# Last pass of a two-layer kernel: the stores of the result move from the sync engine's queue to ScalarE's

## The chip, the cores and the metric

The kernel runs on one core of a Trainium2 chip, as one launch. The metric is its device time in microseconds. All times called "us" below are of that kind; "ns" is marked.

## The reference, cut to what matters

The input `x` is (8, 512, 128, 128) float32, 256 MB, and so is the output.

```python
# layer 0: a 3x3 stride-2 grouped convolution, a gate per channel cluster, then upsampling back
x1 = conv(sx, w_down)                       # (8, 256, 64, 64), "downsampled" in the kernel
labels = kmeans(x1[0]); mu, var = gmm(mean over each cluster); y = sigmoid(...)
up = repeat((1 + y[:, slabel]) * x1, 2, axis=1) * w_up
x = bilinear_up_x2(up) + sx
# layer 1: linear attention in a basis P of 64 cosine products, with norms lamdq, lamdk, lamdv
xP = x P;  WqxP, WkxP, WvxP = Wq xP, Wk xP, Wv xP
out = WvxP @ ((A fatt PT/lamdq + rowsum) / lamdv) + out_bias
return gamma * out + x
```

All that is large in the last pass is: read x again, read the downsampled image, compute per 4 rows of the picture one product that carries both the upsampled image and the attention's result, add x and a shift per channel, and write the result.

## The kernel before

There are four passes, one after another. The first reads x, convolves it with VectorE and projects it with TensorE. Two short ones compute clusters and the mixture, and work out the gates. The last, `second_pass`, begins at some 2070 us. All of the change is in it.

The last pass goes over 8 batches. Each has `UNITS` = 32 units of 4 rows, and a unit is 1 MB of x, read into one of `XBUF` = 8 slots `second_x` by two DMAs of 512 KB, changed in place, and stored by two DMAs of 512 KB. Two units make a chunk of 8 rows, for which 4 to 6 rows of the downsampled image (`second_dd`) are read. Every engine has its own instruction stream, written out by hand; `batches` runs `step(b, u, more)` for every unit, in a loop over seven batches and then once more, unrolled, for the last (there `more` is False). Engines are tied only by semaphores. What each does for unit u:

- The sync engine's queue (SP), `step` at line 1026: on odd u the rows of a later chunk (`load_rows`), then `store(b, u)`, then `load_image` of unit u + 6 (`AHEAD`), which waits on `y_out`, that is until the slot's last store (that of unit u - 2) has landed. `store` (line 1010) waits until VectorE has added the last of four banks of u.
- ScalarE, `step` at line 1299: `stage` (for a few u, small steps of the next batch's attention: copies, a square root at u = 15); on odd u `weight(b, m + 2, 0)`, eight ACTIVATEs (L1257) that interpolate vertically for the chunk after next; `copy(b, u + 1)` (L1278, L1281, L1282), which copies transposed rows from PSUM for GpSimd and the right-hand factor for TensorE; on odd u `weight(b, m + 2, 1)`, eight more. `weight` with 0 waits for the interpolation of an earlier chunk (`interpolated`), since it writes a part buffer that VectorE has read.
- GpSimd: scales the copied rows by the gates into half of the left factor (L964, `second_left`), which TensorE waits for at its first product of the next unit.
- TensorE: four groups of 8 matmuls (L1172) into four PSUM banks `second_o`, one per bank; after the first the transposes of unit u + 1 (L1142, `second_mid_t`), after the second those of L1155; then `stage`, the matmuls of the next batch's attention (none in the last batch).
- VectorE, `step` at line 1465, an order that matters here. `add` n (L1417) takes bank n and adds it to x in the slot. The order is `add` 0, `scale_odd` of unit u + 1 (L964), `add` 1, on even u `frequencies` (L1408), `add` 2, on even u `interpolate` (L1399), `add` 3, then `stage`. So on even units the interpolation is ahead of the last add, whose semaphore `store` waits for. On odd units there is no interpolation.

Of the kernel before, what the change touches and what calls it, by code (L numbers as in the profile page):

```python
# [9 lines left out]
B, C, H, W = 8, 512, 128, 128  # L10
P = 128
T, S = 2, 2
# [36 lines left out]
FREE = 1  # L49
# [823 lines left out]
HALF = ROWS2 // 2  # L873
UNITS = H // HALF
PAIRS = HALF // 2
BANKS = TS
XBUF = 8
# [14 lines left out]
def second_pass(nc, x, cst, p_sb, r_sb, inter, wqk_sb, wv_sb, vx, gam, xd, xps, coef, out):  # L892

    xv = x.rearrange("b (t g s) h w -> b t g s (h w)", t=T, s=S)
    ov = out.rearrange("b (t g s) h w -> b t g s (h w)", t=T, s=S)
    with Scope(nc, "second") as sc:
        xt = [sc.sb(f"x{i}", [P, T, S, HALF, W]) for i in range(XBUF)]
# [30 lines left out]
        y_out = [sc.sem(f"y_out{i}") for i in range(XBUF)]  # L928
# [8 lines left out]
        added = [sc.sem(f"added{i}") for i in range(BANKS)]  # L937
# [20 lines left out]
        def chunk_of(u):  # L958
            return u // 2
# [10 lines left out]
        def batches(eng, step, prologue=None):  # L970

            if prologue:
                prologue()
            with eng.Fori(0, B - 1) as b:
                for u in range(UNITS):
                    step(b, u, True)
            for u in range(UNITS):
                step(B - 1, u, False)

        with nc.Block() as block:  # L980
            @block.sync
            def _(sp):
                def load_rows(b, m):

                    slot, n = m % 2, m % CH2

                    sp.wait_ge(weighted, b * CH2 + m + CHUNK_LEAD - 1)
                    batch = b + m // CH2
                    rows = xd[batch].rearrange("t g n -> g t n")
                    first, last = max(n * DROWS - 1, 0), min(n * DROWS + DROWS + 1, HD)  # L990
                    at = first - (n * DROWS - 1)
                    if n == 0:
                        sp.dma_start(dd[slot][:, :, 0, :], rows[:, :, 0:WD]).then_inc(dd_in[slot], 16)
                    if n == CH2 - 1:
                        sp.dma_start(dd[slot][:, :, HALO - 1, :], rows[:, :, (HD - 1) * WD:HD * WD]
                                     ).then_inc(dd_in[slot], 16)
                    sp.dma_start(dd[slot][:, :, at:at + last - first, :].rearrange("g t h w -> g t (h w)"),
                                 rows[:, :, first * WD:last * WD]).then_inc(dd_in[slot], 16)

                def load_image(b, u, free=True):  # L1000
                    i = u % XBUF
                    if free:

                        sp.wait_ge(y_out[i], (b * (UNITS // XBUF) + u // XBUF) * T * 16 + Y_LEAD)
                    for t in range(T):
                        sp.dma_start(xt[i][:, t, :, :, :].rearrange("g s h w -> g s (h w)"),
                                     xv[b + u // UNITS, t, :, :, u % UNITS * HALF * W:(u % UNITS + 1) * HALF * W]
                                     ).then_inc(x_in[i], 16)

                def store(b, u):  # L1010
                    i = u % XBUF
                    sp.wait_ge(added[BANKS - 1], b * UNITS + u + 1 + FREE)
                    for t in range(T):
                        sp.dma_start(ov[b, t, :, :, u * HALF * W:(u + 1) * HALF * W],
                                     xt[i][:, t, :, :, :].rearrange("g s h w -> g s (h w)")).then_inc(y_out[i], 16)

                def prologue():
                    load_rows(0, 0)
                    load_rows(0, 1)
                    for u in range(AHEAD):  # L1020
                        load_image(0, u, free=False)
                    load_rows(0, 2)
                    for i in range(XBUF):
                        sp.sem_inc(y_out[i], Y_LEAD)

                def step(b, u, more):
                    if u % 2 == 1 and (more or chunk_of(u) < CH2 - 3):
                        load_rows(b, chunk_of(u) + 3)
                    store(b, u)
                    if more or u + AHEAD < UNITS:  # L1030
                        load_image(b, u + AHEAD)

                batches(sp, step, prologue)
                for i in range(XBUF):
                    sp.wait_ge(y_out[i], B * UNITS // XBUF * T * 16 + Y_LEAD)
# [181 lines left out]
            def _(act):  # L1217
# [22 lines left out]
                def weight(b, m, e):  # L1240


                    c, n = m % 2, m % CH2
                    if e == 0:
                        if c == 0:
                            loads = (m // CH2) * (CH2 // 2 + 1) + n // 2 + 1 + 1
                        else:
                            loads = (m // CH2) * (CH2 // 2 + 1) + n // 2 + 1 + (n == CH2 - 1)
                        act.wait_ge(dd_in[c], b * (CH2 // 2 + 1) * 16 + loads * 16)

                        act.wait_ge(mid_turned, (b * CH2 + m) * 2 - 2 + TURN_LEAD)
                        if m > 0:

                            act.wait_ge(interpolated, b * CH2 + m)
                    for r in range(2):
                        for i in range(DROWS):
                            last = nc.scalar.activation(  # L1257
                                (mid[c], part)[r][:, :, 2 * i + 1 - e, :], dd[c][:, :, e + r + i, :], ACT.Copy,
                                scale=row_w[:, 2 * e + r, n * DROWS + i:n * DROWS + i + 1])
                    if e == 1:  # L1260
                        last.then_inc(weighted, 1)

                def place_vt(b, u):

                    a = u % 2
                    act.wait_ge(multiplied, (b * UNITS + u) * BANKS - BANKS + UNIT_LEAD)
                    act.wait_ge(vt_made, b + u // UNITS + 1)
                    for rows, e in ((lo, 0), (hi, 1)):
                        last = nc.scalar.activation(left[a][rows, e:HALF:2, :, :].rearrange("p h n g -> p h (n g)"),
                                                    vt[rows, :].unsqueeze(1).broadcast_to([UV, PAIRS, C]), ACT.Copy)  # L1270
                    last.then_inc(vt_placed, 1)

                def copy(b, u):

                    a = u % 2
                    act.wait_ge(mid_turned, b * UNITS + u + 1 + TURN_LEAD)
                    act.wait_ge(left_made[1], b * UNITS + u + FREE)
                    nc.scalar.activation(mid_copy[hi, :, :, :], mid_t[hi, :, :, :], ACT.Copy).then_inc(mid_copied, 1)  # L1278
                    act.wait_ge(zt_turned, b * UNITS + u + 1 + TURN_LEAD)
                    act.wait_ge(multiplied, (b * UNITS + u) * BANKS - BANKS + UNIT_LEAD)  # L1280
                    nc.scalar.activation(right[a][lo, 0:HALF:2, :], zt_t[lo, 0:PAIRS, :], ACT.Copy)  # L1281
                    nc.scalar.activation(right[a][hi, 1:HALF:2, :], zt_t[hi, 0:PAIRS, :], ACT.Copy  # L1282
                                         ).then_inc(right_made, 1)
                    if u % UNITS < 2:
                        place_vt(b, u)

                def prologue():
                    for b in range(B):
                        act.wait_ge(coef_turned, b + 1)
                        nc.scalar.activation(coef_all[:, b, :], zt_t[:, :, :].rearrange("p n g -> p (n g)"), ACT.Copy  # L1290
                                             ).then_inc(coef_copied, 1)
                    for m in range(2):
                        for e in range(2):
                            weight(0, m, e)
                    for u in range(UNITS):
                        stage(0, u)
                    copy(0, 0)

                def step(b, u, more):
                    m = chunk_of(u)  # L1300
                    if more:
                        stage(b + 1, u)
                    ahead = u % 2 == 1 and (more or m + 2 < CH2)
                    if ahead:
                        weight(b, m + 2, 0)
                    if more or u < UNITS - 1:
                        copy(b, u + 1)
                    if ahead:
                        weight(b, m + 2, 1)

                batches(act, step, prologue)

            @block.vector
# [287 lines left out]
```

## Time and profile before

| | us |
|---|---|
| median of 3 runs | 3865.55 (3852.54 to 3874.26) |
| the profiled execution, its own time | 3863.4 |
| its span | 3861.8 |
| PE busy in the span | 3209.1 (83%) |
| DVE busy | 3018.2 (78%) |
| ACT busy | 1871.3 (48%) |
| POOL busy | 645.3 (17%) |
| second_x stores, KB each | 512 DMAs, 512.0 KB, 5.7 us to landing |
| second_x loads, KB each | 512 DMAs, 512.0 KB, 7.5 us to landing |

PE is TensorE, PEld its weight loads, DVE VectorE, ACT ScalarE, POOL GpSimd, SP the sync engine. A letter q behind an engine (SPq) means its instruction queue: a DMA shows there as long as its issue takes, not as long as the data travel. "A releaser" is what ended an engine's idle time. Busy shares are averages over passes with different limits, so the last pass has to be read by itself.

### The profile page before, as it was taken

The page shows a single profiled execution, that of the slowest core. Times are in us where ns is not written, and L with a number is a line of the kernel's source. Part 1 is how long each engine was busy: PE and PEld are TensorE (multiplying, and loading weights), DVE is VectorE, ACT ScalarE, POOL GpSimd, SP SyncE. Part 2 cuts the span into 40 slices and gives each one's busy share as a digit, 9 for nine tenths or more (in the row PEclk, how much of TensorE's full clock was granted, in tenths as well). Part 3 has the DMA queues.
Part 4 walks back from the last instruction along what each step waited for, and adds up shares of the span by engine and source line. Part 5 has one row for each costly group of instructions (what it writes and reads, how often), then busy time and mean ns, then how long its engine had stood idle before and what let it go on. Part 6 is the DMA issues. An engine that isn't in the chain of part 4 may idle for free. (4 is left out here: it accounts for less than half of the span.)

```text
span 3861.8 us, 68816 instructions
## 1 busy us (share of the span) xinstructions
PE 3209.1 (83%) x23738; PEld 2390.1 (62%) x23738; DVE 3018.2 (78%) x3491; ACT 1871.3 (48%) x4272; POOL 645.3 (17%) x325
## 2 busy tenths in 40 slices
PE   7999999999999745998556887888889887888877
PEld 3454554545455345776334787877778787877777
DVE  5999999999999933113443897979889797979877
ACT  4555555555555310222221555555655556555654
POOL 0000000000000000000000333333333333333333
PEclk9999999999999865998666999999999999999999
DMA  6646556556556212221002899999999999999998
GB/s 275 254 201 259 243 206 264 231 219 264 220 231 265 116 73 98 102 116 44 0 0 78 289 345 322 348 327 346 346 340 343 326 343 337 343 325 347 353 349 305
DMA packets 348925, 945.54 MB, mean 245 GB/s; under 512 B 25937, under 2 KB 58833, under 8 KB 329490
## 3 DMA queue, kind: packets, MB, share of 16 engines
q1 hardware_dynamic: 339346, 907.41, 63.3%
q0 software_dynamic: 9216, 33.56, 2.1%
q8 instruction: 194, 3.18, 0.3%
q14 instruction: 169, 1.38, 0.1%
HBM read 638.90 MB, written 301.99 MB: 244 GB/s over the span
## 5 line engine op out<-in xcount | busy, mean ns | idle before, releaser
L189 DVE SCALAR_TENSOR_TENSOR first_acc<-first_x,first_wd,first_acc 128x1024 f32<-128x1024 f32 (+1 forms) x1088 | 1297.8, 1275 | 57.4 <-ACT first_acc L214 46.0
L1172 PE MATMUL second_o<-second_right,second_left 128*128 128x128 f32 x8192 | 1106.9, 286 | 186.5 <-POOL second_left L964 121.1
L1172 PEld LDWEIGHTS second_o<-second_right,second_left 128*128 128x128 f32 x8192 | 1023.0, 200 | 239.7 <-issue 211.2
L964 POOL TENSOR_TENSOR second_left<-second_mid_copy,second_coef_rep 64x1024 f32<-64x1024 f32 x256 | 610.6, 2385 | 1881.9 <-ACT second_mid_copy L1278 1876.4
L1417 DVE SCALAR_TENSOR_TENSOR second_x<-second_o,second_shift,second_x 128x512 f32<-128x512 f32 x1024 | 734.1, 738 | 233.5 <-PE second_o L1172 231.1
L218 ACT ACTIVATE first_xT<-first_tp 128x512 f32<-128x512 f32 x1024 | 608.3, 597 | 533.6 <-PE first_tp L244 533.0
L244 PE MATMUL first_tp<-all_const,first_x 128*128 128x128 f32 x4096 | 679.4, 291 | 79.8 <-issue 41.5
L244 PEld LDWEIGHTS first_tp<-all_const,first_x 128*128 128x128 f32 x4096 | 441.3, 143 | 461.1 <-issue 444.4
L256 PE MATMUL first_freq<-first_xT,all_p 128*64 128x256 f32 x4096 | 667.4, 407 | 17.7 <-ACT first_xT L218 8.1
L1257 ACT ACTIVATE second_mid<-second_dd,all_inter 128x128 f32<-128x128 f32 x1024 | 327.1, 390 | 386.0 <-DVE second_mid L1399 374.7
L256 PEld LDWEIGHTS first_freq<-first_xT,all_p 128*64 128x64 f32 x4096 | 210.6, 136 | 193.9 <-issue 178.8
L1257 ACT ACTIVATE second_part<-second_dd,all_inter 128x128 f32<-128x128 f32 x1024 | 323.3, 386 | 0.0
L964 DVE TENSOR_TENSOR second_left<-second_mid_t,second_coef_rep 64x1024 f32<-64x1024 f32 x256 | 308.7, 1206 | 5.9 <-PE second_mid_t L1142 4.0
L1142 PE MATMUL second_mid_t<-all_const,second_mid 128*128 128x128 f32 x1024 | 174.2, 297 | 97.7 <-DVE second_mid L1399 97.7
L164 POOL DMA_DIRECT2D downsampled<-first_acc x64 | 34.2, 535 | 1323.4 <-DVE first_acc L189 1120.7
L565 DVE TENSOR_TENSOR gates_ft<-gates_ft,average_mean 128x512 f32<-128x512 f32 x64 | 44.0, 688 | 243.4 <-PE average_mean L517 243.4
L1278 ACT ACTIVATE second_mid_copy<-second_mid_t 64x512 f32<-64x512 f32 x256 | 151.6, 592 | 163.5 <-PE second_mid_t L1142 138.4
L1142 PEld LDWEIGHTS second_mid_t<-all_const,second_mid 128*128 128x128 f32 x1024 | 127.9, 152 | 115.6 <-DVE second_mid L1399 115.6
L1408 DVE TENSOR_TENSOR second_zt<-all_p,second_rr 128x512 f32<-128x512 f32 x128 | 194.5, 1519 | 0.2 <-DVE second_rr L1392 0.2
L540 ACT ACTIVATE average_dT<-average_tp 128x512 f32<-128x512 f32 x128 | 74.9, 597 | 172.5 <-PE average_tp L495 172.5
L1399 DVE TENSOR_TENSOR second_mid<-second_mid,second_part 128x1024 f32<-128x1024 f32 x128 | 154.8, 1209 | 4.3 <-ACT second_part L1257 4.3
L1281 ACT ACTIVATE second_right<-second_zt_t 64x256 f32<-64x256 f32 x256 | 96.5, 377 | 107.7 <-PE second_zt_t L1155 104.4
(215 smaller groups left out, 2327.3 us busy)
## 6 DMA issues: line engine op xcount, KB each, us to landing
second_x<-in_x SPq DMA_DIRECT2D x512, 512.0 KB, 7.5
out<-second_x SPq DMA_DIRECT2D x512, 512.0 KB, 5.7
first_x<-in_x SPq DMA_DIRECT2D x48, 4224.0 KB, 25.3
first_x<-in_x SPq DMA_DIRECT2D x16, 4096.0 KB
second_dd<-downsampled SPq DMA_DIRECT2D x112, 384.0 KB, 6.4
downsampled<-first_acc POOLq DMA_DIRECT2D x64, 512.0 KB, 11.6
average_xd<-downsampled SPq DMA_DIRECT2D x16, 2048.0 KB, 8.4
second_dd<-downsampled SPq DMA_DIRECT2D x16, 320.0 KB, 6.2
```

The costliest lines, as they stand in the source:

```text
L189: nc.vector.scalar_tensor_tensor(out=acc[c][:, :, left:], in0=tap_window(xt[c], (s, dh, dw), OUT1), scalar=wd[:, t, k:k + 1], in1=acc[c][: ...
L218: nc.scalar.activation(xT[slot][:, :, :], tp[slot][:, :, :], ACT.Copy).then_inc(copied[slot], 1)
L244: last = nc.tensor.transpose(tp[slot][:, n * S + s, :], xt[c][:, s, 1 + r + n, :], ident)
L256: last = nc.tensor.matmul(freq_ps[t][n * UV:(n + 1) * UV, 0:S * P], p_sb[:, row, :], xT[slot][:, n * S:(n + 1) * S, :].rearrange("p s g -> ...
L964: return eng.tensor_tensor(left[a][rows, odd:HALF:2, :, :].rearrange("p n (t s) g -> p n t s g", t=T), turned[rows, :, :, :].unsqueeze(3). ...
L1142: last = nc.tensor.transpose(mid_t[:, n, t, :], mid[m % 2][:, t, r:r + 2, :].rearrange("p h w -> p (h w)"), k("ident"))
L1172: last = nc.tensor.matmul(ob[n][:, r, :], left[a][:, r, n, :], right[a][:, r, :], start=True, stop=True)
L1257: last = nc.scalar.activation((mid[c], part)[r][:, :, 2 * i + 1 - e, :], dd[c][:, :, e + r + i, :], ACT.Copy, scale=row_w[:, 2 * e + r, n ...
L1278: nc.scalar.activation(mid_copy[hi, :, :, :], mid_t[hi, :, :, :], ACT.Copy).then_inc(mid_copied, 1)
L1399: nc.vector.tensor_tensor(mid[c][:, :, :, :], mid[c][:, :, :, :], part[:, :, :, :], ALU.add).then_inc(interpolated, 1)
L1408: nc.vector.tensor_tensor(zt[c][:, :, :], p_sb[:, rows, :], rr[:, rows].unsqueeze(2).broadcast_to([P, ROWS2, UV]), ALU.mult).then_inc(zt_m ...
L1417: nc.vector.scalar_tensor_tensor(out=xt[i][:, n // S, n % S, :, :], in0=ob[n][:, :, :], scalar=shift[:, n:n + 1], in1=xt[i][:, n // S, n % ...
```

## The change

`store` leaves the sync engine's stream and enters ScalarE's, with the same wait, the same addresses and the same semaphore. It is the last thing that ScalarE does for a unit. Loads stay where they were.

```diff
--- before.py
+++ after.py
@@ sync engine
-                def store(b, u):
-                    i = u % XBUF
-                    sp.wait_ge(added[BANKS - 1], b * UNITS + u + 1 + FREE)
-                    for t in range(T):
-                        sp.dma_start(ov[b, t, :, :, u * HALF * W:(u + 1) * HALF * W],
-                                     xt[i][:, t, :, :, :].rearrange("g s h w -> g s (h w)")).then_inc(y_out[i], 16)
-
                 def step(b, u, more):
                     if u % 2 == 1 and (more or chunk_of(u) < CH2 - 3):
                         load_rows(b, chunk_of(u) + 3)
-                    store(b, u)
                     if more or u + AHEAD < UNITS:
                         load_image(b, u + AHEAD)
@@ ScalarE
+                def store(b, u):
+                    i = u % XBUF
+                    act.wait_ge(added[BANKS - 1], b * UNITS + u + 1 + FREE)
+                    for t in range(T):
+                        act.dma_start(ov[b, t, :, :, u * HALF * W:(u + 1) * HALF * W],
+                                     xt[i][:, t, :, :, :].rearrange("g s h w -> g s (h w)")).then_inc(y_out[i], 16)
+
                 def step(b, u, more):
                     ...
                     if ahead:
                         weight(b, m + 2, 1)
+                    store(b, u)
```

## Rows read from the trace of the kernel before

**Rows 1.** The page: busy per engine, granted clock and DMA share in 40 slices.
```profile
PE 3209.1 (83%) x23738; PEld 2390.1 (62%) x23738; DVE 3018.2 (78%) x3491; ACT 1871.3 (48%) x4272; POOL 645.3 (17%) x325
PEclk9999999999999865998666999999999999999999
DMA  6646556556556212221002899999999999999998
```
**Rows 2.** Waits, 2200 to 3861 us: waiter, releaser, us in total, times, longest.
```profile
ACT second_mid L1257 <- DVE second_mid L1399: 358.1, 107, 3.9
...
PE second_o L1172 <- POOL second_left L964: 118.5, 57, 4.3
...
ACT second_mid L1257 <- DMA second_dd<-downsampled: 3.6, 1, 3.6
```
**Rows 3.** The chain of waits, 2733 to 2746 us: start, duration, engine and tile.
```profile
2733.16 1.14 DVE second_mid L1399
2734.70 0.97 ACT second_mid L1257 x3
...
2737.52 2.37 POOL second_left L964
2739.99 1.13 PE second_o L1172 x8
...
2745.85 1.14 DVE second_mid L1399
```
**Rows 4.** Timeline of one pair of units: start, duration, engine, operation [idle before, releaser].
```profile
2626.38 1.21 DVE L1399 TENSOR_TENSOR second_mid<-second_mid,second_part 128x1024 f32<-128x1024 f32 x1
2627.52 0.74 DVE L1417 SCALAR_TENSOR_TENSOR second_x<-second_o,second_shift,second_x 128x512 f32<-128x512 f32 x1
...
2627.68 1.28 ACT L1257 ACTIVATE second_mid<-second_dd,all_inter 128x128 f32<-128x128 f32 x4 [3.52 <-DVE second_mid L1399]
...
2628.28 1.32 SPq L1014 DMA_DIRECT2D out<-second_x  x2
...
2630.14 0.59 ACT L1278 ACTIVATE second_mid_copy<-second_mid_t 64x512 f32<-64x512 f32 x1
...
2630.81 2.36 POOL L964 TENSOR_TENSOR second_left<-second_mid_copy,second_coef_rep 64x1024 f32<-64x1024 f32 x1 [5.56 <-ACT second_mid_copy L1278]
...
2633.27 1.13 PE L1172 MATMUL second_o<-second_right,second_left 128*128 128x128 f32 x8 [0.16 <-issue]
2633.95 1.32 SPq L1014 DMA_DIRECT2D out<-second_x  x2
...
2634.88 0.59 ACT L1278 ACTIVATE second_mid_copy<-second_mid_t 64x512 f32<-64x512 f32 x1 [0.88 <-PE second_mid_t L1142]
...
2639.05 1.21 DVE L1399 TENSOR_TENSOR second_mid<-second_mid,second_part 128x1024 f32<-128x1024 f32 x1
```
**Rows 5.** Issues of DMAs by line: ns min/median/max, first and last start; landing times.
```profile
L1014 SPq DMA_DIRECT2D out<-second_x x512: 534/614/1877, 2138.6 to 3856.6; - x171
...
DMA to landing us min/median/max: 3.1/5.7/10.1
L1006 SPq DMA_DIRECT2D second_x<-in_x x482: 604/1028/2137, 2200.0 to 3823.5; - x161
L164 POOL DMA_DIRECT2D downsampled<-first_acc x64: 531/531/723, 84.8 to 1358.3; - x64
```
**Rows 6.** Timeline at two other places: the loop's end, and unit 15.
```profile
2567.53 0.59 ACT L1278 ACTIVATE second_mid_copy<-second_mid_t 64x512 f32<-64x512 f32 x1 [4.12 <-issue]
2667.61 0.42 ACT L1232 ACTIVATE second_lam<-second_lam 128x256 f32<-128x256 f32 x1 [5.44 <-DVE second_lam L1341]
```
**Rows 7.** Last batch: a first product, L1399's starts, one window (PE, ..., clock, DMA, GB/s).
```profile
3702.10 1.84 PE L1172 MATMUL second_o<-second_right,second_left 128*128 128x128 f32 x8 [2.10 <-POOL second_left L964]
L1399 DVE TENSOR_TENSOR second_mid<-second_mid,second_part x15: 1207/1209/1210, 3656.1 to 3841.6; 128x1024 f32<-128x1024 f32 x15
3660.00:3850.00 190.00, 145.14 (x1102) 139.13 (x1102) 146.41 (x174) 106.19 (x306) 69.91 (x30) 0.92 0.95 333
```

## The prediction

> **What bounds the kernel now.** I began with the page, which says only that no engine is full and that in the last pass the DMA engines look nearly full [rows 1]. Averages don't tell which wait counts, so next came the waits of the last pass. The reader is to see two things in them [rows 2]. ScalarE waits 107 times, 358 us in all, for VectorE's interpolation before it can start `weight`; and TensorE waits for GpSimd's left factor. No wait on an x load appears; the one DMA wait is 3.6 us. The chain of waits ties the two together [rows 3]: interpolation (VectorE), weights (ScalarE), the copy of the transposed rows, scaling (GpSimd), the first product of the even unit (TensorE), and from there VectorE's adds to the next interpolation. It is a closed cycle over two units. The timeline gives its length: interpolations start at 2626.38 and 2639.05, so 12.67 us a pair of units [rows 4]. So although ScalarE is busy for 48% of the span, its work from the end of an interpolation to the copy is on the path, and its idle time lies ahead of that.
>
> **The pieces of the cycle** [rows 4]. The interpolation ends at 2627.59. ScalarE, idle for 3.52 us, starts its weights at 2627.68, its copy at 2630.14, GpSimd starts at 2630.81, TensorE at 2633.27, and 5.78 us later the next interpolation begins. The last add of the same even unit starts at 2627.52 and ends at 2628.26, that is after the weights have started. SP issues the two stores at 2628.28, for 1.32 us. They cost the cycle nothing now, since SP has nothing on it.
>
> **What the change adds, even units.** In ScalarE's stream the store of even unit u stands ahead of the weights of step u + 1. Behind it are queued weights, the copy, the right factor; GpSimd, TensorE and then VectorE wait for these. Two things are new on the path.
> - The wait for the last add: from the weights' old start, 2627.68, to 2628.28: 0.60 us.
> - The issue of two DMAs by ScalarE. The trace has none of ScalarE. Nearest rows: the same store on SP takes 534/614/1877 ns, median in the middle, and a pair of them with its gaps 1.32 us; loads, issued right behind others, have a median of 1028 ns; a DMA issued by GpSimd has 531 ns [rows 5]. Bounds for the pair: 0 (if what follows weren't held up) and 1.06 (2 x 531) from below, 2.06 (2 x 1028) from above. I take the same transfer's own, 1.32, and 0.05 to restart, since the transfer doesn't change.
>
> Together 1.97 us per pair, a new cycle of 14.64 us. Nothing in the rest of the cycle shrinks: what follows is a row of engines each waiting for the one before.
>
> **Odd units.** Their stores were issued at 2633.95, when ScalarE ends its second weights (eight ACTIVATEs of 0.39 us after the copies). ScalarE was then idle for 0.88 us until the next copy at 2634.88 [rows 4]. In the new order the store takes it to some 2635.35, so the copy and GpSimd are 0.45 us later. That unit's first product was ready at about 2638.0 and has to end only when the interpolation does (2640.26) for the transposes behind it; it has 1.1 us of room. I cost odd stores at nothing. If the issue took 2.06 instead, that room would be used up and no more.
>
> **What is taken from SP.** Its stores' issue, 1.32 us a unit, on a queue that nobody waits for: 0. `load_image` for unit u + 6 no longer stands behind `store(u)`; it starts when the store of unit u - 2 has landed, about a unit earlier. Loads already come six units ahead and no add waits for them [rows 2]: 0. No transfer is added or taken away.
>
> **How many pairs pay.** The last pass has 128 pairs. Each of the seven looped batches has 13 in which ScalarE waits for the interpolation as above, and the last batch, without the attention's steps, about 13 more: 104. 104 x 1.97 = 205 us.
> - At u = 15 ScalarE waits 5.44 us for VectorE's sums, ending at 2667.61, after the last add of unit 14 [rows 6]. The issue hides in that wait: 0.1 us, 7 times, 1 us.
> - Around the loop's end ScalarE pays the 2 us for the pair, and then also the issue of unit 31's store ahead of its 4.12 us of "issue" (the jump) [rows 6], after which the copy starts the chain again: 2.0 + 1.4 = 3.4, 7 times, 24 us.
> - In the pair behind it TensorE's and ScalarE's own work fills the time: 0.
>
> **TensorE's clock.** In the last batch TensorE is idle for 2.1 us ahead of the even unit's first product. There it runs in part at 1.2 GHz: the product of 8 takes 1.84 us in place of 1.13, the granted clock of the stretch is 0.92, and interpolations are (3841.6 - 3656.1) / 14 = 13.25 us apart, 0.58 above 12.67 [rows 4, 7]. With a clock of 0.92 some half of the pairs can have such a stretch, so one costs about 0.58 / 0.5 = 1.1 us. In the looped batches that gap is now mostly under 1 us, filled by the next batch's matmuls (0.16 in rows 4). I estimate from the gaps of one such batch: with 2 us more in every pair, some 8 of the 13 have gaps of 2.0 to 2.3 and behave as the last batch does now (0.55 each), and 5 have over 3 us (1.1 each): 9.9 per batch, 69 us for seven; less what falls there already, about 6. The last batch goes from half to all: 13 x 0.55 = 7. Sum 70 us. Bounds: 0, and 104 x 1.1 = 114.
>
> **The sum.** 205 + 24 + 1 + 70 = 300 us on the profiled execution's own 3863.4 (span 3861.8): 4163 us. The median shown is 2 us above that execution, which is nothing here.
>
> **Rivals.**
> - *Issues collide* (slower still). SP's loads are now released by landings. With the odd store issued about 7.8 us after the even one and landing 5.7 us later [rows 5], SP would issue two loads, 2 x 1.03 us, at some 14.2 after the even store; the next even store comes at 14.6. If one issue had to wait for the other, ScalarE would lose up to 2.06 us a pair, on average half: 104 x 1.03 = 107, so 4270 us. Against it: with a 13% lower data rate (12.67 / 14.64) landings may come sooner than 5.7 us, and the loads be through. The Trainium skill, "Perfetto Trace Analysis", section on the HWDGE DMA instruction, says that the descriptor generator is shared by the issuing sequencers and that waiting for its lock is inside the profiled duration. By that rule the collision is real whenever the two overlap; no row of before can show it, since SP alone issues there.
> - *ScalarE's issue holds nothing up.* Only the wait on the last add stays: 104 x 0.60 = 62, loop ends 5, clock about 25: 3955 us. For it only that the rows of before have no DMA on ScalarE; against it that SP's second DMA starts only when the first has ended, 1.32 for a pair [rows 4].
> - *Not slower: the DMA engines set the pace.* Their share is 0.95 and the rate 333 GB/s [rows 7], and nine tenths in most slices [rows 1]. Were the pace that of the transfers, with eight slots as the buffer between, ScalarE's 2 us would be lost in the waiting for data, and earlier loads would keep the DMA engines fuller: 3863 us. It decides from the point at which an add waits for a load. There is none [rows 2], which speaks against it. The Trainium skill, "Perfetto Trace Analysis", DMA Optimizations, holds that one engine for inputs and another for outputs may make sense in a loop; its promise is this case, and the trace shows no wait that it would shorten.
>
> **How the numbers follow.** Forecast 70% (its own range 4090 to 4235: issue of 1.06 to 1.7 us a pair and the clock between 20 and 114), collisions 17%, no holding up 7%, transfers set the pace 6%. A measurement of this kernel can tell about 0.5% from no change. Faster by more than that 0.02, within it 0.04, slower 0.94. The range from 4020 to 4290 takes in the collisions and what lies between the forecast and the second rival.
>
> **What would show it.** ScalarE's queue should have 512 stores of about 0.61 us each, the even ones right behind the last add and ahead of L1257. Waits: L1257's wait for L1399 should nearly vanish, TensorE's wait for GpSimd should grow by about 200 us. Interpolations should be 14.6 us apart, 15.7 where the clock falls. The loads on SP should start by landings of stores. I am wrong if the pairs stay at 12.7, if the stores on ScalarE take 1 us and more, or if x loads become a releaser of VectorE.

## The result, and the profile after

The changed kernel takes 4217.29 us (median of 4 runs, 4212.77 to 4224.52) against 3862.46 us before. The ratio is 1.0914, 95% interval 1.0895 to 1.0934: 9% slower. The forecast was 4163 us. The profiled execution took 4212.77 us (span 4211.1), so 349 us have to be found between two spans.

First the page of the changed kernel, to lay beside [rows 1]: busy times, granted clock and DMA share, queues, and the issues of the last pass.

```profile
PE 3352.7 (80%) x23738; PEld 2539.0 (60%) x23738; DVE 3037.3 (72%) x3491; ACT 1878.1 (45%) x4272; POOL 652.2 (15%) x325
PEclk9999999999998679966589889888988988988888
DMA  6565555656562133200258788887887788877886
q1 hardware_dynamic: 200082, 638.95, 41.1%
q10 hardware_dynamic: 139264, 268.47, 17.6%
second_x<-in_x SPq DMA_DIRECT2D x512, 512.0 KB, 5.2
out<-second_x ACTq DMA_DIRECT2D x512, 512.0 KB, 5.0
```

The stores have a queue of their own (q10). Stores and loads both land sooner, and the DMA engines are less busy: transfers are not what got worse. ScalarE's busy time has not changed; what it issues is not counted as busy. TensorE's 23738 records take 144 us more, and the granted clock of the whole execution is 0.880 where it was 0.919. VectorE's busy time hardly moves.

Second, the waits from 2200 us on (waiter, releaser, us in total, times, longest), to lay beside [rows 2].

```profile
ACT second_mid L1249 <- issue: 517.2, 99, 6.7
...
PE second_o L1164 <- POOL second_left L964: 322.5, 98, 5.1
```

L1249 is what L1257 was. Its idle time has a new releaser: no longer the interpolation but "issue", ScalarE's own queue. That is how these DMAs show in front of a compute instruction of the same engine. TensorE's wait for GpSimd went from 118.5 to 322.5 us, by 204, where some 200 were foreseen.

Third, a pair of units in the timeline of the changed kernel (start, duration, engine, operation, idle before and releaser), to lay beside [rows 4].

```profile
2752.73 1.21 DVE L1399 TENSOR_TENSOR second_mid<-second_mid,second_part 128x1024 f32<-128x1024 f32 x1
...
2753.86 0.74 DVE L1417 SCALAR_TENSOR_TENSOR second_x<-second_o,second_shift,second_x 128x512 f32<-128x512 f32 x1
...
2754.76 1.25 ACTq L1283 DMA_DIRECT2D out<-second_x  x2
...
2756.27 1.28 ACT L1249 ACTIVATE second_mid<-second_dd,all_inter 128x128 f32<-128x128 f32 x4 [4.72 <-issue]
...
2759.42 2.34 POOL L964 TENSOR_TENSOR second_left<-second_mid_copy,second_coef_rep 64x1024 f32<-64x1024 f32 x1 [7.82 <-ACT second_mid_copy L1270]
...
2760.44 0.57 ACTq L1283 DMA_DIRECT2D out<-second_x  x1
2760.47 0.97 ACT L1249 ACTIVATE second_mid<-second_dd,all_inter 128x128 f32<-128x128 f32 x3
2761.17 0.56 ACTq L1283 DMA_DIRECT2D out<-second_x  x1
2761.35 1.27 ACT L1249 ACTIVATE second_part<-second_dd,all_inter 128x128 f32<-128x128 f32 x4
...
2761.86 2.05 PE L1164 MATMUL second_o<-second_right,second_left 128*128 128x128 f32 x8 [3.26 <-POOL second_left L964]
...
2768.97 1.21 DVE L1399 TENSOR_TENSOR second_mid<-second_mid,second_part 128x1024 f32<-128x1024 f32 x1
```

The whole case is in these rows. The interpolation ends at 2753.94, the last add at 2754.60, ScalarE issues the two stores at 2754.76, for 1.25 us, and starts its weights at 2756.27: 2.33 us after the interpolation's end, where it was 0.09. That is +2.24 us. From there to TensorE's first product it takes 5.59 us, as it did (2627.68 to 2633.27 in [rows 4]). The product itself runs at the lower clock, 2.05 us for 1.13, and from its start to the next interpolation 7.11 us pass in place of 5.78: +1.33. Sum: 12.67 + 2.24 + 1.33 = 16.24 us, which is the distance of the two interpolations.

Fourth, the issues by line (ns min/median/max), to lay beside [rows 5].

```profile
L1283 ACTq DMA_DIRECT2D out<-second_x x512: 541/549/1677, 2135.7 to 4206.0; - x171
...
L1006 SPq DMA_DIRECT2D second_x<-in_x x512: 539/543/2198, 2037.3 to 4152.4; - x171
```

**Where the 349 us are.** From the 128 starts of the interpolation in each trace, before and after (distance of neighbours, mean over the kind):

| pairs | before | after | difference, times their number |
|---|---|---|---|
| 105 ordinary ones | 12.93 | 16.01 | 323 |
| 7 across the loop's end | 14.35 | 16.34 | 14 |
| 7 at units 0 to 2 of the looped batches | 19.11 | 20.54 | 10 |
| 7 at units 14 to 16 | 16.14 | 16.43 | 2 |

Of the ordinary pairs' 3.08 us, 2.24 are the wait and the issue (105 x 2.24 = 235 us): from the interpolation's end to the weights it is 0.12 us before and 2.37 after, as a mean over the 105. The other 0.84 us (88 us) I put down to the clock. Nearly all of it lies behind the first product (5.92 us before, 6.71 after), and the filling below bears this out. The pairs at units 0 to 2 scatter from 15.2 to 22.7 us in the changed kernel, so their 10 us are not firm.

### The profile page after: what moved, and what is told of

Same layout as the page of the kernel before. It is cut to its first block, busy times and chain, and to the rows that moved or that the text cites. A ratio compares the mean times of both kernels' runs of the same rounds, so it can differ in the third digit from the quotient of the medians.

```text
span 4211.1 us, 68956 instructions
## 1 busy us (share of the span) xinstructions
PE 3352.7 (80%) x23738; PEld 2539.0 (60%) x23738; DVE 3037.3 (72%) x3491; ACT 1878.1 (45%) x4272; POOL 652.2 (15%) x325
## 4 chain that ended last, share of the span: by engine, by line
PE 21%; issue 19%; POOL 8%; ACT 2%; DVE 1%; ACTq 1%; POOLq 0%; DVEq 0%
PE second_o L1164 14%; POOL second_left L964 8%; PE second_mid_t L1134 3%; PE second_st L1082 2%; PE second_zt_t L1147 1%; PE second_st L1045 1%; ACT second_mid_copy L1270 1%; ACT second_left L1261 1%; DVE second_x L1417 0%; ACTq L1283 0%; PE second_zt_t L1175 0%; ACT second_part L1249 0%; ACT second_mid L1249 0%; DVE second_zt L1408 0%; PE second_st L1074 0%
## 5 line engine op out<-in xcount | busy, mean ns | idle before, releaser
L1164 PE MATMUL second_o<-second_right,second_left 128*128 128x128 f32 x8192 | 1218.0, 305 | 415.7 <-POOL second_left L964 331.6
L1164 PEld LDWEIGHTS second_o<-second_right,second_left 128*128 128x128 f32 x8192 | 1141.8, 220 | 464.2 <-issue 432.2
L964 POOL TENSOR_TENSOR second_left<-second_mid_copy,second_coef_rep 64x1024 f32<-64x1024 f32 x256 | 617.4, 2412 | 2223.1 <-ACT second_mid_copy L1270 2184.9
L1249 ACT ACTIVATE second_mid<-second_dd,all_inter 128x128 f32<-128x128 f32 x1024 | 328.7, 392 | 596.0 <-issue 537.2
L1249 ACT ACTIVATE second_part<-second_dd,all_inter 128x128 f32<-128x128 f32 x1024 | 324.9, 388 | 0.0
L964 DVE TENSOR_TENSOR second_left<-second_mid_t,second_coef_rep 64x1024 f32<-64x1024 f32 x256 | 309.9, 1210 | 20.1 <-PE second_mid_t L1134 18.1
L1134 PE MATMUL second_mid_t<-all_const,second_mid 128*128 128x128 f32 x1024 | 208.0, 340 | 72.5 <-DVE second_mid L1399 72.4
L1134 PEld LDWEIGHTS second_mid_t<-all_const,second_mid 128*128 128x128 f32 x1024 | 157.3, 177 | 89.9 <-DVE second_mid L1399 89.9
L1408 DVE TENSOR_TENSOR second_zt<-all_p,second_rr 128x512 f32<-128x512 f32 x128 | 178.0, 1391 | 0.2 <-DVE second_rr L1392 0.2
L1399 DVE TENSOR_TENSOR second_mid<-second_mid,second_part 128x1024 f32<-128x1024 f32 x128 | 156.8, 1225 | 4.3 <-ACT second_part L1249 4.3
```

The lines of the kernel that those rows point to most:

```text
L964: return eng.tensor_tensor(left[a][rows, odd:HALF:2, :, :].rearrange("p n (t s) g -> p n t s g", t=T), turned[rows, :, :, :].unsqueeze(3). ...
L1134: last = nc.tensor.transpose(mid_t[:, n, t, :], mid[m % 2][:, t, r:r + 2, :].rearrange("p h w -> p (h w)"), k("ident"))
L1164: last = nc.tensor.matmul(ob[n][:, r, :], left[a][:, r, n, :], right[a][:, r, :], start=True, stop=True)
L1249: last = nc.scalar.activation((mid[c], part)[r][:, :, 2 * i + 1 - e, :], dd[c][:, :, e + r + i, :], ACT.Copy, scale=row_w[:, 2 * e + r, n ...
L1399: nc.vector.tensor_tensor(mid[c][:, :, :, :], mid[c][:, :, :, :], part[:, :, :, :], ALU.add).then_inc(interpolated, 1)
L1408: nc.vector.tensor_tensor(zt[c][:, :, :], p_sb[:, rows, :], rr[:, rows].unsqueeze(2).broadcast_to([P, ROWS2, UV]), ALU.mult).then_inc(zt_m ...
```

## The experiments

All edits are in the last pass. "Before" ran with them on the same chip, at 3861 to 3866 us.

**Even units' stores alone, odd units' alone.** The other half stays on the sync engine's queue.

```diff
+                    if u % 2 == 0:        # ScalarE, first kernel; u % 2 == 1 in the second
                         store(b, u)
```

> Only the even units' stores are on ScalarE; those of odd units are back on the sync engine's queue. Theory: the whole cost hangs on the even units, whose store stands between the interpolation and ScalarE's weights (0.66 us for the last add, 1.25 for two issues, 0.33 around them: 2.24 us a pair) and so takes TensorE's clock with it. Then the time is that of the changed kernel, 4190 to 4220 us, pairs of 14.9 and 16.2 us. Rival: every pair of DMA issues in ScalarE's stream costs it time, the odd ones too, so half of the 355 us goes: about 4040 us.

> Only the odd units' stores are on ScalarE. Theory: they fall where ScalarE waited for the transposes anyway, so 3860 to 3885 us, pairs of 12.7 us as before. Rival (each issue costs): about 4040 us.

Even ones alone: 4191.36 us, ratio 1.086 (1.083 to 1.0889), ordinary pairs 16.05 us. Odd ones alone: 3896.02 us, ratio 1.0088 (1.0063 to 1.0114), ordinary pairs 13.20. With 256 issues on ScalarE in either, the rival's 4040 us is missed by both. The even units' stores carry 329 of the 355 us. The odd ones, which I had put at nothing, were not free: 34 us when alone, and 11 us above the expected range. The timeline of that kernel shows one place where they cost.

```profile
2636.77 2.05 DVE L1427 SCALAR_TENSOR_TENSOR second_x<-second_o,second_shift,second_x 128x512 f32<-128x512 f32 x3
...
2638.99 1.28 ACTq L1292 DMA_DIRECT2D out<-second_x  x2
...
2640.44 0.59 ACT L1279 ACTIVATE second_mid_copy<-second_mid_t 64x512 f32<-64x512 f32 x1 [1.54 <-PE second_mid_t L1143]
...
2641.11 2.40 POOL L964 TENSOR_TENSOR second_left<-second_mid_copy,second_coef_rep 64x1024 f32<-64x1024 f32 x1 [3.02 <-ACT second_mid_copy L1279]
...
2641.81 2.25 DVE L1418 TENSOR_TENSOR second_zt<-all_p,second_rr 128x512 f32<-128x512 f32 x1
```

The last add of this odd unit ends at 2638.82, so the store is issued at 2638.99, the copy is some 0.6 us late, and so is GpSimd's scaling. The product had the room that I gave it. What had none was VectorE's L1408 (here L1418): it takes 2.25 us in place of 1.58, its median in the kernel before, because it meets more of GpSimd's operation in this pair. The pair is 13.36 us long. The median of L1418 over that kernel is 1.58 us still; in 15 of the 105 ordinary pairs it takes over 2 us, before in none. The last section has more on this.

**All stores on ScalarE, one unit late.**

```diff
-                    store(b, u)
+                    if u > 0:
+                        store(b, u - 1)
+                    if u == UNITS - 1:
+                        store(b, u)
```

> All stores on ScalarE, but at the end of unit u it stores unit u - 1 (and unit 31 at the batch's end): the last add is long done, and on even units the issue falls into the 3.5 us in which ScalarE waits for the interpolation. Theory: 3860 to 3890 us, L1249 waits for the interpolation again. Rival (it is the number of issues on ScalarE, 512, or the two queues together, that cost): 4150 us or more.

3880.66 us, ratio 1.0048 (1.0033 to 1.0062), ordinary pairs 12.95 us. The same 512 issues on the same queue cost 19 us and not 355, and these lie around the loop's end: pairs at units 0 to 2 take 20.69 us in place of 19.11, those across the end 15.14 in place of 14.35. Its timeline:

```profile
2610.84 0.38 ACT L1273 ACTIVATE second_right<-second_zt_t 64x256 f32<-64x256 f32 x1 [0.60 <-PE second_zt_t L1147]
2611.02 0.55 ACTq L1283 DMA_DIRECT2D out<-second_x  x1
2611.22 0.38 ACT L1274 ACTIVATE second_right<-second_zt_t 64x256 f32<-64x256 f32 x1
2611.72 0.55 ACTq L1283 DMA_DIRECT2D out<-second_x  x1
...
2615.11 1.28 ACT L1249 ACTIVATE second_mid<-second_dd,all_inter 128x128 f32<-128x128 f32 x4 [3.51 <-DVE second_mid L1402]
```

The issues lie beside ACTIVATEs and in the time in which ScalarE waits for the interpolation. That wait is back, 3.51 us (3.52 in [rows 4]). So neither the second queue nor issuing from ScalarE is the main cost; the place is.

**The wait alone, the issue alone, and the add moved forward.** In the first, the kernel before gets ScalarE's wait at the end of each unit and nothing else. In the second, ScalarE issues the odd units' stores two units late, when their add is long done, between the interpolation's semaphore and the first weight; the even units' stores stay with the sync engine. In the third, the changed kernel's VectorE does the even unit's last add ahead of the interpolation.

```diff
+                    act.wait_ge(added[BANKS - 1], b * UNITS + u + 1 + FREE)   # wait alone, ScalarE
...
+                    if late is not None:                                      # issue alone, in weight(), late = u - 2
+                        store(b, late)
...
-                        if n == 2 and u % 2 == 0 and (more or m + 1 < CH2):   # add forward, VectorE
+                        if n == 3 and u % 2 == 0 and (more or m + 1 < CH2):
                             interpolate(b, m + 1)
```

> The kernel before, with all stores on the sync engine's queue, but ScalarE waits at the end of each unit for the last add, and issues nothing. Theory: 0.66 us plus 0.05 to 0.1 a pair on the cycle, 104 pairs: 75 us, and some 30 to 60 us of clock: 3965 to 4000 us. Rival (the issue alone costs, the wait is met): 3865 us. Rival (the wait makes nearly all): 4150 us or more.

> ScalarE issues the stores of odd units only, two units late, so that their add is long done, and does it between the interpolation's wait and the first weight ACTIVATE; even units' stores are on the sync engine's queue. So the path gets an issue of two DMAs and no new wait. Theory: 1.25 us of issue and 0.26 to 0.35 us around it, 1.5 to 1.6 us a pair, 104 pairs: 160 us, and 40 to 80 us of clock: 4060 to 4110 us, pairs of 14.2 to 14.3 us or 15.5. Rival (an issue on ScalarE's queue is overlapped with its ACTIVATEs, and only the wait cost): 3870 to 3900 us.

> The changed kernel, but VectorE does the last add of an even unit ahead of the interpolation and not behind it, so that ScalarE issues the store while the interpolation runs. Theory: the interpolation is 0.7 us later, and the issue (0.16 + 1.25 + 0.26 us after the add) ends 0.4 us after the interpolation's end (1.14 us + 0.09): weights start 1.1 us later than in the kernel before, in place of 2.24 us. 105 pairs: 120 us and 20 to 60 us of clock: 4000 to 4050 us. Rival (the order doesn't matter, the issue costs anywhere in ScalarE's stream): 4200 us.

Wait alone: 3962.81 us, ratio 1.0264 (1.0237 to 1.029), just below the expected range; median pair 13.50. Issue alone: 4071.03 us, 1.0539 (1.05 to 1.0578); median pair 14.58, the clock in it. Add forward: 3971.17 us, 1.0264 (1.0224 to 1.0305); median pair 13.80. The timelines show each term: the starts of the interpolation and of the weights, first with the wait alone, then with the issue alone.

```profile
2666.96 1.21 DVE L1400 TENSOR_TENSOR second_mid<-second_mid,second_part 128x1024 f32<-128x1024 f32 x1
...
2669.01 1.28 ACT L1257 ACTIVATE second_mid<-second_dd,all_inter 128x128 f32<-128x128 f32 x4 [4.28 <-PE second_mid_t L1142]
```

```profile
2669.75 1.21 DVE L1413 TENSOR_TENSOR second_mid<-second_mid,second_part 128x1024 f32<-128x1024 f32 x1
...
2671.16 1.26 ACTq L1245 DMA_DIRECT2D out<-second_x  x2
...
2672.47 1.28 ACT L1267 ACTIVATE second_mid<-second_dd,all_inter 128x128 f32<-128x128 f32 x4 [4.17 <-PE second_mid_t L1143]
```

From the interpolation's start to that of the weights 2.05 and 2.72 us pass, where the kernel before has 1.30 [rows 4]: 0.75 us for the wait (0.76 by the median pairs, 13.50 against 12.74) and 1.42 for the issue. They add up to 2.17, against 2.24 in the changed kernel. In both groups the profile names TensorE's transposes as the releaser of the weights. That misleads: the weights start right behind the last add (2668.83, its end in the first kernel) and behind the issue (2672.42 in the second). With the add forward the expected 1.1 us a pair came out (13.80 against 12.74); the total was below what I expected, since none of the clock was lost: granted 0.922 over the execution, as in the kernel before (0.916 to 0.918). The order of two instructions on VectorE is worth 246 us here (4217.29 - 3971.17).

**Filling TensorE's gap.** At the end of odd units TensorE multiplies the identity into the first bank, which the next product overwrites.

```diff
+                    if u % 2 == 1 and (more or u < UNITS - 1):
+                        pe.wait_ge(added[0], b * UNITS + u + 1 + FREE)
+                        for n in range(...):   # fill_clock 16 or 30, fill_short 8 or 12
+                            nc.tensor.matmul(ob[0][:, n % HALF, :], k("ident"), k("ident"), start=True, stop=True)
```

> The changed kernel, and TensorE multiplies the identity by itself 16 or 30 times (0.11 us each) at the end of odd units, into the first bank, already read, where it idles for 3.3 us before the even unit's first product. Theory: about 1.1 us of each pair is the 1.2 GHz stretch (pairs of 14.9 where there is none, mean 16.0). With the gap filled the clock stays up in most pairs: mean 15.0, 100 us less, some 4110 to 4140 us. Rival (the pair is 16.0 for another reason, such as contention of the two DMA queues): 4217 us or more.

> As fill_clock, with 8 or 12 extra matmuls in place of 16 or 30. The trace of fill_clock showed that one such matmul is two records of 0.12 us, so that 16 took 3.84 and 30 some 7 us, more than the gap: there the clock stayed up, but the first product came late. 8 take 1.9 us and 12 take 2.9, inside gaps of 3.2 to 4.0. Theory (1.2 GHz stretches make 1.1 us of the 16.0 us pair): pairs of 14.9 to 15.0, 105 us less than the changed kernel: 4100 to 4140 us. Rival (something else makes it): 4200 us or more.

The long filling took 4342.02 us, ratio 1.123 (1.1191 to 1.1269): a miss. The clock is granted in full in every ordinary pair, but the filling is longer than the gap (16 matmuls take 3.84 us), and from the start of GpSimd's scaling to the first product 4.16 us pass on average in place of 2.58. So the miss is one of my sizing. The short one took 4132.52 us, ratio 1.0703 (1.0674 to 1.0732): 85 us less than the changed kernel, with more matmuls. These are the windows from 2600 to 3700 us of the changed kernel and of this one (us, PE, PEld, DVE, ACT, POOL busy, clock, DMA share, GB/s).

```profile
2600.00:3700.00 1100.00, 848.34 (x6402) 786.09 (x6401) 796.43 (x969) 539.56 (x1518) 323.60 (x134) 0.88 0.82 282
```

```profile
2600.00:3700.00 1100.00, 935.08 (x7894) 860.00 (x7895) 800.03 (x984) 555.52 (x1566) 340.05 (x138) 0.98 0.82 288
```

The clock rises from 0.88 to 0.98. The median ordinary pair is 14.94 us, with the clock at 1.00 in it: 2.20 above the 12.74 of before, which is the wait and the issue and next to nothing else. In the last batch, where the gap is longest (4.1 us on average in the changed kernel, 2.8 in the looped ones), the median pair falls from 15.9 to 14.6 us. In three pairs of each looped batch, at units 16 to 22, where TensorE does most for the next batch, they are 16.2 with the filling, which is too long there; so 85 us came back and not the 105 expected.

**Opening the cycle.** A second buffer for what the weights hand to the interpolation, so that they wait for the interpolation two chunks back. To make room for it, small tensors of the next batch's attention (`m1`, `xp`, `qk`, `ms`) share the memory of others; the excerpt below leaves that out.

```diff
-        part = sc.sb("part", [P, T, ROWS2, WD])
+        part = [sc.sb(f"part{i}", [P, T, ROWS2, WD]) for i in range(2)]
...
-                        if m > 0:
-                            act.wait_ge(interpolated, b * CH2 + m)
+                        if m > 1:
+                            act.wait_ge(interpolated, b * CH2 + m - 1)
```

It was run with the stores as before (two_parts_sp), as in the changed kernel (two_parts_act), and one unit late on ScalarE (two_parts_lag).

> The kernel before, with two buffers for what the weights write for the interpolation (room made by letting five small tensors share others' bytes), so that ScalarE's weights for a chunk wait for the interpolation two chunks back and not one: the cycle interpolation, weights, copy, GpSimd, TensorE, adds is opened. Theory (the cycle was the bound of the pair): pairs fall from 12.7 to what TensorE needs with the next batch's matmuls, 11.7 to 12.8: 3770 to 3830 us. Rival (the transfers, whose share is 0.95 to 1.02, set the pace): 3850 to 3865 us.

> The changed kernel with two buffers for the weights' part, as in two_parts_sp: ScalarE no longer waits for the interpolation, but still for the last add of the even unit ahead of its weights. Theory: the store makes a cycle of its own (last add, issue, weights, copy, GpSimd, product, adds), so opening the other one gives nothing: 4190 to 4220 us. Rival (only the interpolation's cycle matters, and with it open the store is hidden as well): 3800 to 3900 us.

> Two part buffers, all stores on ScalarE one unit late as in lag_one_unit. The weights wait for nothing but their rows. Theory: neither cycle is left. In two_parts_sp ScalarE waited 238 us for the rows of the downsampled image, whose load stands behind a store's wait on the sync engine's queue; here no store is ahead of it. But the issue of 1.25 us is now in a ScalarE stream with less idle time. 3770 to 3830 us; if it falls below 3799, the sync engine's queue is worth freeing once ScalarE isn't held up. Rival (with more issued by ScalarE it becomes the bound): above 3860 us.

3799.49 us, ratio 0.9827 (0.9792 to 0.9861); 4218.91 us, 1.0924 (1.0893 to 1.0956); 3817.71 us, 0.9894 (0.9863 to 0.9926). The first shows that the cycle, and not the transfers, set the pace of the kernel before: ordinary pairs fall from 12.93 to 12.50 us on average. The second tells most about the change: with the interpolation out of the way it still takes the same 4218 us. The store brings a cycle of its own, from the last add over issue, weights, copy, GpSimd and products back to the add. It takes the place of the old one. The third doesn't fall below the first, so moving the stores off the sync engine's queue gains nothing there either: ordinary pairs are 12.39 us, but those at units 0 to 2 take 19.74 us in place of 16.02. In the first of the three the weights had a new releaser, and this gave the last experiment.

```profile
ACT second_mid L1258 <- DMA second_dd<-downsampled: 237.5, 82, 5.5
```

**Rows loaded half a pair earlier**, on top of two_parts_sp.

```diff
-                    if u % 2 == 1 and (more or chunk_of(u) < CH2 - 3):
+                    if u % 2 == 0 and (more or chunk_of(u) < CH2 - 3):
                         load_rows(b, chunk_of(u) + 3)
```

> two_parts_sp, with the downsampled rows of a later chunk loaded by the sync engine's queue at even units and no longer at odd ones, half a pair earlier. In two_parts_sp ScalarE's weights waited 238 us for these rows. Theory: that wait goes, but behind it stands TensorE, which in the units with the next batch's matmuls needs 12.86 us a pair anyway: 20 to 60 us less than two_parts_sp, 3740 to 3780 us. Rival (the transfers or TensorE were the bound already): 3795 to 3805 us.

3758.77 us, ratio 0.9739 (0.9722 to 0.9755). That wait falls from 237.5 to 18.2 us, ordinary pairs are 12.12 us on average (12.50 in two_parts_sp), and this kernel beats both: 2.6% below before and 11% below the changed one. What ScalarE waits for now is TensorE.

```profile
ACT second_mid_copy L1279 <- PE second_mid_t L1143: 356.9, 214, 4.2
```

## Why the prediction was right, and where a size was off

- *The cycle that bounds the last pass* was named rightly, and two_parts_sp bears it out: opened, it gives 67 us.
- *Even units carry the cost:* right in kind (4191 us with these alone). The direct term was 1.97 us a pair and measured 2.24. Issue was taken as 1.32 and is 1.25. The difference lies at its ends: 0.16 us from the add's end to the issue, where SP had 0.02, and 0.26 from the issue's end to the first ACTIVATE, where I had put 0.05. Times 105 that is 28 us.
- *The clock:* forecast 70 us, measured 88. The kind was right, the size of one stretch at 1.2 GHz was not: 1.1 us taken, 1.33 in the pair shown above. Filled, the gap gives 85 us back.
- *Odd units at nothing:* right for the ordinary pairs of the changed kernel, since there the odd stores are issued while the weights still run (2760.44 and 2761.17 above), and the ordinary pairs of even_only are no shorter (16.05 against 16.01 us). That even_only is 26 us faster lies in its pairs at units 0 to 2 (15.62 against 20.54 us); why, no run shows. By itself it failed: 34 us in odd_only. In the pair shown there the step that broke is the room of 1.1 us. I measured it to TensorE's product and overlooked that VectorE's L1408 runs beside GpSimd. But this explains only a part: the 15 pairs with an L1408 of over 2 us make some 10 us, while the ordinary pairs together gain 28 and those at units 0 to 2 another 15. The rest stays open.
- *The loop's end and the pair behind it:* 24 + 0 forecast, 14 + 10 measured. That the sum is the same is luck.
- *Sum:* 300 forecast, 349 measured. The forecast's own range of 4090 to 4235 us was drawn too tight for what it names: an issue of 1.06 to 1.7 us and a clock term of 20 to 114 us, with the other terms as they stood, give some 4086 to 4246.
- *Issues collide:* no. In the changed kernel 167 of 512 store issues overlap in time with an x load's issue on SP, and their median is 0.55 us, the same as that of the others. Of the 105 pairs of issues on the path, 22 do, at a median of 1.26 us for the two (1.25 over all). On this the traces differ from the rule that I weighed (the Trainium skill, "Perfetto Trace Analysis", section "DMA Instruction — HWDGE (DVE, Sync)", that the generator is locked for exclusive use and the wait for the lock is in the profiled duration); the measurement decides. SP's queue now issues its loads with no store ahead, at a median of 543 ns where it took 1028.
- *ScalarE's issue holds nothing up:* no for a store that stands alone in front of idle ScalarE (1.42 us in issue_only), yes for one behind queued ACTIVATEs (lag_one_unit).
- *Transfers set the pace:* no. With pairs at 12.12 us the same transfers get through in two_parts_rows.

## What to carry to other kernels

Before a DMA is put into a compute engine's stream, ask what it waits for and what stands behind it; the engine's busy share (48% here) says nothing on that, and the same 512 issues cost 355 us in one place and 19 us one unit later. An instruction that waits for the last link of a loop and stands ahead of its first link closes a new cycle: look for the order in which the producer (here VectorE) makes the two things. A gap on TensorE can cost twice, once as a wait and once as clock (here 2.24 and 0.84 us a pair).

## What the runs showed of the hardware

- ScalarE's queue runs ahead of its engine. At 2760.44 a store is issued while seven of the eight ACTIVATEs that stand ahead of it in the program are still to run (to 2762.6). No idle time of ScalarE stands beside the issue there, while it costs 1.25 + 0.16 + 0.26 us where the wait ahead of it has drained the engine.
- VectorE's L1408 takes 0.68 us when GpSimd's L964 is not running, and in the kernel before 0.61 us plus 0.94 for each us of overlap (a line fitted through the 128 instances; 0.59 and 0.97 in odd_only). It practically stands still meanwhile: in 123 of the 128 it starts while L964 runs, and each of these ends 0.55 us behind L964's end. The Trainium skill, "SBUF — State Buffer", section "Who interferes with whom", says that a VectorE instruction with two inputs in SBUF contends with a GpSimd instruction that reads SBUF, and that the port pair they share is an exclusive lock; the trace agrees.
- One 128x128 float32 matmul that the program issues is two records of about 0.12 us (16 issued: x32 and 3.84 us in fill_clock). So the groups of 8 at L1172, which I called 8 matmuls, are four of the program's.
- The chain of waits of the changed kernel says mostly "issue" (62.7% in the stretch from 2740 to 2775 us), where the timeline shows the wait for the last add and the two stores. The timeline has to be read there.
